# Bias and gate of the gated outputs on ScalarE instead of VectorE, in a two-layer conditioned transformer on one core

## What is computed

```python
# layer 0
x = x + gate_a[:, None] * (attn(modulate(_ln(x), shift_a, scale_a)) @ W_proj + b_proj)
x = x + cross_attn(_ln(x), _ln(context)) @ W_cproj + b_cproj
x = x + gate_m[:, None] * (gelu(modulate(_ln(x), shift_m, scale_m) @ W_mlp1 + b_mlp1) @ W_mlp2 + b_mlp2)
# layer 1: self-attention and cross-attention with rotary positions, then an MLP; no gates
```

## Time and profile before

| | us |
|---|---|
| median of 3 runs | 382.94 |
| lowest, highest | 380.88, 384.89 |
| profiled execution, device time | 385.06 |
| its span, first to last instruction | 383.3 |
| PE, DVE, ACT, POOL busy | 363.0, 301.7, 254.5, 100.6 |

### The profile page before, as it was taken

One profiled execution on the slowest core, in us unless ns is written; L12 is line 12 of the kernel. 1 busy time (PEld: TensorE's weight loads), 2 busy tenths in 40 slices (PEclk: granted clock), 3 DMA queues, 4 the chain that ended last, 5 costly groups with the idle time before them and its releaser, 6 DMA issues.

```text
span 383.3 us, 12514 instructions
## 1 busy us (share of the span) xinstructions
PE 363.0 (95%) x5090; PEld 260.6 (68%) x5090; DVE 301.7 (79%) x809; ACT 254.5 (66%) x513; POOL 100.6 (26%) x120
## 2 busy tenths in 40 slices
PE   7699999999999999999999999999999899999996
PEld 3485687677776776657654567666677577886776
DVE  5985989999999998947999839997799747875302
ACT  2525965578676987889453797378766945688551
POOL 6920310142020201125351234343413401031130
PEclk9966999999999999999999999999999957999999
DMA  8673244005221360014050140403140404000003
GB/s 208 259 240 93 78 140 167 9 27 186 84 88 43 127 219 5 3 32 169 2 193 6 29 168 7 169 5 106 65 168 4 168 8 159 8 3 3 2 0 111
DMA packets 19757, 34.13 MB, mean 89 GB/s; under 512 B 2740, under 2 KB 7988, under 8 KB 19700
## 3 DMA queue, kind: packets, MB, share of 16 engines
q1 hardware_dynamic: 19268, 33.24, 25.2%
q10 hardware_dynamic: 432, 0.09, 0.2%
HBM read 6.51 MB, written 1.05 MB: 20 GB/s over the span
## 4 chain that ended last, share of the span: by engine, by line
PE 55%; DVE 4%; ACT 3%; DMA 3%; SPq 3%; issue 2%; ACTq 0%; DVEq 0%
PE ps_ao L1058 11%; PE ps_misc L999 8%; PE ps_misc L1028 6%; PE ps_misc L1109 6%; PE ps_misc L1087 6%; PE ps_misc L1025 6%; PE ps_misc L935 3%; PE ps_misc L1094 3%; DVE maxima L690 3%; PE ps_misc L1068 2%; PE ps_misc L1007 2%; ACT PT L882 2%; DMA Ks<-Kl 2%; DMA Ks<-Kh 1%; SPq L537 1%
## 5 line engine op out<-in xcount | busy, mean ns | idle before, releaser
L690 DVE TENSOR_REDUCE maxima<-ps_misc 128x4 f32<-128x512 f32 (+1 forms) x256 | 153.5, 664 | 17.6 <-PE ps_misc L1025 17.1
L882 ACT ACTIVATE PT<-ps_misc 128x512 f32<-128x512 f32 (+1 forms) x256 | 131.7, 606 | 24.0 <-PE ps_misc L1028 22.7
L1058 PE MATMUL ps_ao<-PT,V 120*18 120x128 f32 (+1 forms) x2048 | 70.5, 282 | 0.5 <-ACT PT L882 0.5
L1025 PEld LDWEIGHTS ps_misc<-Ks,Qd 32*128 32x128 f32 x1024 | 41.9, 197 | 30.8 <-issue 11.3
L1025 PE MATMUL ps_misc<-Ks,Qd 32*128 32x128 f32 (+1 forms) x1024 | 53.4, 298 | 8.5 <-DMA Ks<-Kl 3.3
L1058 PEld LDWEIGHTS ps_ao<-PT,V 120*18 120x18 f32 (+1 forms) x2048 | 52.6, 101 | 7.4 <-issue 2.3
L1028 PEld LDWEIGHTS ps_misc<-Qd,Ks 32*128 32x128 f32 (+1 forms) x1024 | 38.0, 186 | 21.5 <-issue 13.7
L752 POOL TENSOR_SCALAR vareps<-mv 128x4 f32<-128x4 f32 (+1 forms) x28 | 6.4, 228 | 170.9 <-DVE mv L595 170.6
L1028 PE MATMUL ps_misc<-Qd,Ks 32*128 32x128 f32 (+1 forms) x1024 | 48.7, 287 | 1.5 <-DVE maxima L690 0.8
L866 ACT ACTIVATE xnT<-ps_misc,vec 128x128 f32<-128x128 f32 x80 | 30.1, 462 | 15.6 <-PE ps_misc L935 15.5
L999 PE MATMUL ps_misc<-xnT,Wr 128*128 128x512 f32 x72 | 37.5, 641 | 1.8 <-ACT xnT L866 1.6
(11 more groups left out here) (83 smaller groups left out, 449.7 us busy)
## 6 DMA issues: line engine op xcount, KB each, us to landing
Qd<-Qh SPq DMA_DIRECT2D x32, 256.0 KB
Ks<-Kh SPq DMA_DIRECT2D x16, 256.0 KB, 2.9
Qd<-Ql SPq DMA_DIRECT2D x16, 256.0 KB
Ks<-Kh SPq DMA_DIRECT2D x16, 240.0 KB, 2.4
Ks<-Kl SPq DMA_DIRECT2D x8, 256.0 KB, 3.0
Ks<-Kl SPq DMA_DIRECT2D x8, 240.0 KB, 2.5
x<-x_in SPq DMA_DIRECT2D x4, 256.0 KB, 6.0
W<-weights SPq DMA_DIRECT2D x2, 512.0 KB, 5.0
```

What stands on the lines that cost most here:

```text
L690: dve.tensor_reduce(maxima[:, h, st.b % HB, c, :], bank(use + c)[:, 0:NG * ns].rearrange("p (n k) -> p n k", n=NG), AX_X, ALU.max, negate= ...
L882: act.activation(PT[0:ns, k % PSLOTS, c, :, :].rearrange("p n t -> p (n t)"), bank(use + c)[0:ns, :], ACT.Exp, scale=SCALE).then_inc(S["pr ...
L1025: ins = pe.matmul(bank(st.use + c)[:, n * ns:(n + 1) * ns], queries, keys, start=True, stop=True)
L1058: last = pe.matmul(ps_ao[32 * c:32 * c + PAIR, block * P:(block + 1) * P], heads[:, at:at + PAIR], PT[0:ns, k % PSLOTS, c, n, :], start=no ...
```

## The change

The eight gate steps leave VectorE's list and enter ScalarE's. Each is now four ScalarE activations of 128x128 with the function Identity, which compute `value * gate + bias * gate`; scale and added vector are per-feature operands. The product bias * gate is made once, in two new small VectorE instructions behind the last modulation vectors (`vec.1`). Gate steps wait for these products, for the output's matmuls and for the buffer in yT_sb, as before. The lists of TensorE, GpSimd and SyncE are the same step for step, and those of VectorE and ScalarE are the same apart from the gates. BANK is drawn anew: 592 of its 750 numbers differ, though many only swap names; 58 of the 750 uses follow another use in their bank than before.

```diff
-GATES = "dve"
+GATES = "act"
+ADD_A, ADD_M = NV, NV + 1
...
+                    if part:
+                        dve.wait_ge(S["vec_ready"], NV)
+                        for v, gate, name in ((ADD_A, GATE_A, "o0"), (ADD_M, GATE_M, "b2_0")):
+                            dve.tensor_scalar(vec[:, :, v], vec[:, :, gate], bcol(name), None,
+                                              ALU.mult).then_inc(S["adds_ready"], 1)
...
-                        for b in range(CB):
-                            c = st.s * CB + b
-                            ins = dve.tensor_scalar(yT_sb[:, n % 2, b * P:(b + 1) * P], src[:, b * P:(b + 1) * P],
-                                                    add, vec[:, c, gate:gate + 1], ALU.add, ALU.mult)
-                        ins.then_inc(S["y_ready"], 1)
...
+                        act.wait_ge(S["adds_ready"], 2)
+                        act.wait_ge(S["misc_filled"], filled(source))
+                        if n >= 2:
+                            act.wait_ge(S["misc_filled"], filled(f"yT.{gated[n - 2]}"))
+                        src = bank(plan.at["pe", source].use)
+                        for b in range(CB):
+                            c = st.s * CB + b
+                            ins = act.activation(yT_sb[:, n % 2, b * P:(b + 1) * P], src[:, b * P:(b + 1) * P],
+                                                 ACT.Identity, scale=vec[:, c, gate:gate + 1],
+                                                 bias=vec[:, c, add:add + 1])
+                        ins.then_inc(S["y_ready"], 1)
```

One line of ScalarE's list shows the kind of place where gates now stand (the end of MLP unit m2 and of m3):

```diff
-        xT.m2 aT.7 qhi.9 h.m2.1 h.m2.2 khi.9 h.m2.0
-        h.m2.3 mT.8.0 xT.m3 h.m3.3 mT.8.1 h.m3.1 h.m3.2 h.m3.0 xT.10 mT.9.0 score.8.0 score.8.1 qhi.10 v.10 xT.11
+        xT.m2 aT.7 qhi.9 h.m2.1 h.m2.2 khi.9 h.m2.0 h.m2.3 gate.m2 mT.8.0 xT.m3 h.m3.3 mT.8.1 h.m3.1 h.m3.2 h.m3.0
+        gate.m3 xT.10 mT.9.0 score.8.0 score.8.1 qhi.10 v.10 xT.11
```

More of the change, by code:

```diff
@@ L139 @@
         max.0.1 max.0.2 max.0.3 qlo.2 klo.2 max.1.0 klo.3 cstats.1 max.1.1 qlo.3 cstats.0 cstats.2 max.1.2 max.1.3
[L140 to L153, removed]
+        cln.0 norm.0.1 norm.0.0 max.2.0 cln.1 max.2.1 norm.1.0 max.2.2 upd.0 max.2.3 stats.4 norm.1.1 max.3.0 klo.4
@@ new lines @@
+        ln.4 max.3.1 upd.1 stats.5 max.3.2 ln.5 qlo.4 max.3.3 klo.5 cln.2 norm.2.0 cstats.3 qlo.5 norm.2.1 max.4.0
+        max.4.1 max.4.2 max.4.3 upd.2 stats.6 norm.3.0 norm.3.1 max.5.0 ln.6 max.5.1 max.5.2 max.5.3 upd.3 qlo.6
+        norm.4.0 norm.4.1 stats.7 klo.6 cln.3 ln.7 upd.4 stats.m0 max.6.0 ln.m0 qlo.7 klo.7 norm.5.0 max.6.1
+        max.6.2 norm.5.1 max.6.3 max.7.0 upd.5 stats.m1 ln.m1 max.7.1 upd.m0 stats.8 max.7.2 ln.8 max.7.3 q.8
+        upd.m1 stats.9 k.8 norm.6.0 norm.6.1 ln.9 norm.7.0 upd.6 stats.m2 max.8.0 ln.m2 norm.7.1 q.9 max.8.1 k.9
@@ L154 @@
+        max.14.3 norm.13.0 norm.13.1 max.15.0 max.15.1 upd.12 max.15.2 stats.m4 max.15.3 ln.m4 upd.13 norm.14.1
+        norm.14.0 stats.m5 ln.m5 upd.14 stats.m6 ln.m6 norm.15.0 norm.15.1 upd.15 stats.m7 ln.m7 upd.m6 upd.m5
+        upd.m4 upd.m7""",
     "act": """
@@ L156 @@
         score.0.1 qhi.3 score.0.2 mT.1.0 score.0.3 copy.0.0 copy.0.1 score.1.0 mT.1.1 score.1.1 cT.0 aT.0 score.1.2
[L157 to L160, removed]
@@ L166 @@
[L166 to L170, removed]
@@ L171 @@
-        score.14.2 mT.15.0 score.14.3 aT.13 score.15.0 mT.15.1 copy.14.1 score.15.1 xT.m4 score.15.2 copy.15.0
-        aT.14 score.15.3 xT.m5 copy.15.1 h.m4.3 h.m4.0 h.m4.2 xT.m6 h.m5.0 aT.15 h.m4.1 h.m5.2 h.m5.3 h.m5.1 h.m6.0
-        h.m6.3 xT.m7 h.m6.1 h.m6.2 h.m7.3 h.m7.0 h.m7.1 h.m7.2""",
+        copy.1.0 score.1.3 gate.0 copy.1.1 v.4 mT.2.0 v.3 khi.4 aT.1 mT.2.1 score.2.0 gate.1 score.2.1 xT.4 mT.3.0
+        cT.1 qhi.4 score.2.2 score.2.3 xT.5 khi.5 copy.2.0 score.3.0 qhi.5 mT.3.1 copy.2.1 score.3.1 aT.2 v.5
@@ new lines @@
+        score.3.2 mT.4.0 copy.3.0 score.3.3 gate.2 score.4.0 copy.3.1 mT.4.1 score.4.1 score.4.2 aT.3 copy.4.0
+        score.4.3 gate.3 xT.6 mT.5.0 cT.2 qhi.6 copy.4.1 mT.5.1 score.5.0 khi.6 v.6 aT.4 score.5.1 cT.3 score.5.2
+        xT.7 copy.5.0 khi.7 qhi.7 score.5.3 xT.m0 copy.5.1 h.m0.3 h.m0.2 h.m0.0 mT.6.0 aT.5 v.7 h.m0.1 score.6.0
+        gate.m0 mT.6.1 score.6.1 xT.m1 score.6.2 h.m1.3 copy.6.0 h.m1.0 h.m1.2 h.m1.1 mT.7.0 xT.8 score.6.3 gate.m1
+        mT.7.1 score.7.0 copy.6.1 score.7.1 qhi.8 score.7.2 khi.8 copy.7.0 aT.6 score.7.3 xT.9 v.8 copy.7.1 v.9
@@ new lines @@
+        xT.m2 aT.7 qhi.9 h.m2.1 h.m2.2 khi.9 h.m2.0 h.m2.3 gate.m2 mT.8.0 xT.m3 h.m3.3 mT.8.1 h.m3.1 h.m3.2 h.m3.0
+        gate.m3 xT.10 mT.9.0 score.8.0 score.8.1 qhi.10 v.10 xT.11 score.8.2 copy.8.0 mT.9.1 khi.10 score.8.3
+        score.9.0 score.9.1 copy.8.1 score.9.2 khi.11 aT.8 qhi.11 copy.9.0 score.9.3 copy.9.1 v.11 mT.10.0 aT.9
+        khi.12 xT.12 mT.10.1 score.10.0 score.10.1 qhi.12 copy.10.0 mT.11.0 score.10.2 xT.13 khi.13 score.10.3
+        mT.11.1 score.11.0 copy.10.1 score.11.1 khi.14 score.11.2 aT.10 qhi.13 copy.11.0 mT.12.0 v.13 score.11.3
@@ new lines @@
+        copy.11.1 score.12.0 v.12 xT.14 aT.11 mT.12.1 score.12.1 score.12.2 qhi.14 mT.13.0 copy.12.0 v.14
+        score.12.3 xT.15 copy.12.1 khi.15 mT.13.1 score.13.0 score.13.1 score.13.2 copy.13.0 score.13.3 mT.14.0
+        qhi.15 copy.13.1 score.14.0 mT.14.1 score.14.1 v.15 aT.12 copy.14.0 score.14.2 mT.15.0 score.14.3 aT.13
+        score.15.0 mT.15.1 copy.14.1 score.15.1 xT.m4 score.15.2 copy.15.0 aT.14 score.15.3 xT.m5 copy.15.1 h.m4.3
+        h.m4.0 h.m4.2 xT.m6 h.m5.0 aT.15 h.m4.1 h.m5.2 h.m5.3 h.m5.1 h.m6.0 h.m6.3 xT.m7 h.m6.1 h.m6.2 h.m7.3
@@ L174 @@
+        h.m7.0 h.m7.1 h.m7.2""",
     "pool": """
@@ L334, in block_kernel @@
         silu = sb("silu", [P, 3, B])
-        vec = sb("vec", [P, B, NV])
+        vec = sb("vec", [P, B, NV + 2])
         x = sb("x", [P, STREAMS, CB, D])
@@ L903, in _ @@
                         ins.then_inc(S["attT_ready"], 1)
+                    elif st.kind == "gate":
+                        source = f"h2.{own}" if st.mlp else f"o.{own}"
+                        add = ADD_M if st.mlp else ADD_A
+                        gate, n = spec_of(st)["gate"], gated.index(own)
+                        act.wait_ge(S["adds_ready"], 2)
[9 more added lines that the diff above has]
+                        ins.then_inc(S["y_ready"], 1)
                     elif st.kind == "h":
```

35 lines of the change are left out of this document (14 added, 21 removed), and 2 rows, old and new, of the table BESIDE.

## The result

Over 20 runs of each, on the same chip, the changed kernel took 391.25 us (median; 384.48 to 397.75) and the kernel before 383.80 us (379.84 to 387.16). Single executions wander by several us, so every ratio here is taken over the faster executions of each kernel, those within 1.5% of its fastest; it is **1.0151, 95% interval 1.0107 to 1.0194**: slower by 5.8 us (4.1 to 7.4). The forecast was 386.5, a ratio of 1.0093.

A forecast was written before the change was run, and what follows sets the result against it. PE was busy 95%, so each gate's cost depended on who waits for it. The terms 0.5 + 1.3 + 1.05 + 0.95 - 0.25 = +3.55 us on the median of 382.94 gave 386.5 us, range 383.0 to 391.5.

The forecast's parts named there:

- The cost of a gate: Each gate step on ACT: four activations take 1.50 us, by the row of xT; on DVE a step took 1.36 us.
- Gates 0 to 3: The first four gates, mostly covered by ACT's idle time there: together -0.25 us.
- What was said of gate.0: yT.0 comes some 0.3 us later and a bank wait in max.2.3 goes; between -0.1 and +0.2, taken as 0.
- What was said of gate.1: PE's wait of 0.46 us in score.2.1 goes, but its first bank may start up to 0.4 later: -0.25 us.
- The rival that DVE was the brake: PE follows DVE, so moving gates gives time back: 381.4 us, or 378.7 if more gates gain; chance 0.16.
- Gate m0: At 150.45 us the gate holds ACT ahead of mT.6.1 and score.6.1, whose bank PE's max.7.1 needs: +0.5 us.
- Gate m1: The gate queues behind score.6.3 on ACT and PE's yT.m1, directly behind q.8, waits for it: +1.3 us.
- Gate m2: On ACT xT.m3 stands behind the gate, so PE's h.m3.3 starts later: +1.05 us.
- Gate m3: The gate holds ACT to 213.7 us, so xT.10 and then PE's q.10 come later: +0.95 us.
- The shorter and the longer gate move all four in the direction, by the size and at the places that the queue argument says: At m0 to m3, PE stands directly behind ACT and pays for its queue: 0.5, 1.3, 1.05 and 0.95 us.
- What takes it back: No slack swallows the delays; DMA waits at 182 and 306 move along; new bank waits were taken as 0.
- The clock rival: Added PE idle time at yT.m1, h.m3.3 and q.10 lowers its clock, costing about 5 us: 391.5 us; chance 0.13.

The follow-up runs named there:

- old banks: The changed kernel with the bank table BANK of the kernel before: 391.23 us, ratio 1.016 to the kernel before.
- the two runs of this half: Against the kernel before, only gates 0 to 3 on ACT, m0 to m3 left on DVE, measured twice: 381.74 us (0.990) and 384.18 us (1.003).
- the repeat's ratio: The kernel with only gates 0 to 3 on ACT, run again: 384.18 us, ratio 1.003 to the kernel before.
- the MLP half: Against the kernel before, only gates m0 to m3 on ACT, gates 0 to 3 left on DVE: 390.74 us, ratio 1.018.
- The shorter: The changed kernel with each gate as one activation of 128x512 instead of four of 128x128, changing part of the result: 386.10 us, ratio 1.009 to the kernel before.
- the longer gate: The changed kernel with the four activations at m0 to m3 done twice, first into a spare tile: 404.07 us, ratio 1.048 to the kernel before.
- its repeat: The changed kernel run again as it is: 391.78 us, ratio 1.021 to the kernel before.
- fillers: The changed kernel with useless matmuls ahead of PE's waits at yT.m1, yT.m2, h.m3.3, yT.m3 and q.10: 389.33 us, ratio 1.017 to the kernel before.
- the other order: The changed kernel with yT.m1 behind value.6.3, yT.m2 behind h.m3.1 on PE, and xT.m3 ahead of gate.m2 on ACT: 393.11 us, 1.028 to the kernel before.

## Why the prediction was right in kind and short in size

*The cost of a gate* was taken from the row of `xT`: 1.50 us, measured 1.51. The Trainium skill, VectorE: DVE Perf Modes, section on the TRN2 errata, from which I had an estimate of 1.00 us for four, is off here: 478 ns for one at L909, and 1.51 us for four.

*Gates 0 to 3*, taken as -0.25: the stretch around them gives -0.28, which is within noise, and 0.17 comes back ahead of `max.7.1`, together -0.11. That the size agrees is partly luck. What was said of gate.0 shows: `yT.0` comes 0.4 later and the bank wait behind it goes. What was said of gate.1 does not: the wait of 0.46 in `score.2.1` was to go, and the step still takes 1.05 us against 1.10 (nor is the bank that the gate reads its first; it is its third). Timeline of PE of the changed kernel at `score.2.1`:

```profile
74.69 1.05 PE L1037 MATMUL ps_misc<-Qd,Ks 32*128 32x128 f32 x16
```

`yT.1` is 0.25 earlier all the same, and 0.19 of that arises ahead of `mT.2.1` and not with the old banks. The rival that DVE was the brake is refuted by the traces of the two runs of this half and the repeat's ratio, and by the MLP half, which carries the loss.

*Gate m0*, +0.5 with +0.4 more at worst: 0.63, at the bank of `score.6.1` where the prediction put it. *Gate m1*, +1.3: 1.34. *Gate m2*, +1.05: 1.00. *Gate m3*, +0.95: 1.00. The shorter and the longer gate move all four in the direction, by the size and at the places that the queue argument says.

*The step that failed* is in "What takes it back": "the DMA waits at 182 and 306 hang on steps that move along", taken as 0. At 306 that held (`q.10` to `max.14.0` takes 93.16 us against 93.13). At 182 it did not: `max.8.0` comes 0.72 later than its surroundings, the largest part of the 1.03 by which the traced 4.58 exceeds the forecast 3.55. The steps of ACT, POOL and the queue do move along, the transfer itself is late: it is issued 10.5 to 11.1 us behind the start of `yT.m1` with and without the delay, and lands 14.4 us behind it instead of 13.6 to 13.9. From the DMA view of the changed kernel, the 9 us that end there, queues and issues with their KB and median us to landing:

```profile
q14 instruction: 1, 0.01, 0.2%
...
Ks<-Kl SPq DMA_DIRECT2D x1, 256.0 KB, 3.9
```

The same view of the kernel with only m0 to m3 on ACT, which has no instruction load of that queue there:

```profile
Ks<-Kl SPq DMA_DIRECT2D x1, 256.0 KB, 3.0
```

The late landing goes with the place of this load. In the changed kernel, its repeat, and those with old banks, fillers or short gates, the load starts 5.0 us ahead of the landing whenever the transfer was issued, and `yT.m1` to `max.8.0` takes 14.46 to 14.49 us. With only gates 0 to 3 moved it runs 7 to 7.5 us ahead, in the kernel before and with only m0 to m3 moved there is none in those 10 us, and the stretch takes 13.66 to 13.93. With the doubled gates and with the other order it lies 4.4 us ahead, and the wait at `max.8.0` is 1.12 and 0.96, between the two groups. The DMA view of the half us that ends 0.5 us before `max.8.0`, in the changed kernel and then in the kernel before (packets, MB, share of 16 engines), shows how the transfer ends:

```profile
q1 hardware_dynamic: 6, 0.01, 6.3%
```

```profile
q1 hardware_dynamic: 35, 0.05, 26.4%
```

In the changed kernel the share is that of one of the 16 DMA engines, and it stays so to the end: one engine alone moves the last packets, one behind the other, when the others are done. That fits a load that held this one engine up. But that the load is the cause is argued from where it lies; no run moved it by itself.

*From 4.58 to 5.8.* The traced places leave 1.2 us of the measured difference, which its interval (4.1 to 7.4) doesn't require; the intervals of the repeat (5.1 to 10.8) and of m0 to m3 alone do require more than their places give. Time at low clock is the candidate: over 37 of the faster executions of the kernel before, the span falls by some 2 us for each 0.01 of mean granted clock, and the mean was 0.977 there against 0.976, 0.962 and 0.973 in the changed kernel, its repeat and the one with old banks, and 0.964 with m0 to m3 alone. But the kernel before itself has means of 0.971 to 0.981 from one set of runs to another. Whether the change really lowers the clock stays open.

*The clock rival*, at 391.5, had a second low stretch between 165 and 230 as its sign. The two profiles of the changed kernel have none. The one with the old banks has three, behind `max.8.0`, `h.m3.3` and `q.10`, and the one with the short gate has one, behind `max.8.0`; behind longer waits it came with the doubled gate and the other order. So the rival is not needed for the traced 4.58 us, and it is not excluded as a part of what lies beyond them.

*The chances*: slower by over 1% came true, the interval begins at 1.0107. It had been given 0.47, a little less than a change of under 1% (0.48): the sum without the missing term lay just under that bound.
